# A tower of two mixture-of-experts layers on one core: side-by-side spreads and plain turns in the second experts, a few steps moved between engines

## What is computed

```python
h = tokens(x)        # interpolate by 4, windows of 64, |FFT| of a polynomial and a gaussian, soft minimum
h = h + attention0(layernorm(h))
h = h + experts0(layernorm(h))      # 16 experts, top 2
h = h + attention1(layernorm(h))    # 8 heads with a positional part
h = h + experts1(layernorm(h))      # 8 experts, top 2, gelu; its core:
logits = tokens @ router_w.T;  probs = softmax(logits);  rw, re = top_k(probs, 2);  rw = rw / rw.sum()
combine = zeros(N, 8).at[rows, re].set(rw)
for e in range(8):
    y = gelu(tokens @ w1[e] + b1[e]) @ w2[e] + b2[e]
    out = out + combine[:, e:e+1] * y      # out starts as tokens
```

## Time and profile before

| | |
|---|---|
| time, three runs | 739.51 us (738.17 to 740.50) |
| the profiled execution | 737.55 us, of which the span from first to last instruction is 735.8 us |
| mean granted PE clock | 0.983 |
| PE | 645.7 us busy (88%), 5070 matmuls |
| DVE | 570.9 us (78%) |
| ACT | 502.1 us (68%) |
| POOL | 334.1 us (45%) |
| L1861 and L1839 | 18.0 us each in the second experts |
| L1851 / L1874 | 9.6 us / 8.8 us |

### The profile page before, as it was taken

One profiled execution on the slowest core, in us unless ns is written; L12 is line 12 of the kernel. 1 busy time (PEld: TensorE's weight loads), 2 busy tenths in 40 slices (PEclk: granted clock), 3 DMA queues, 4 the chain that ended last, 5 costly groups with the idle time before them and its releaser, 6 DMA issues. The chain is left out here.

```text
span 735.8 us, 16590 instructions
## 1 busy us (share of the span) xinstructions
PE 645.7 (88%) x5070; PEld 353.0 (48%) x5070; DVE 570.9 (78%) x1647; ACT 502.1 (68%) x1264; POOL 334.1 (45%) x417
## 2 busy tenths in 40 slices
PE   4557998999999988899999988799888988888896
PEld 4524655666666653233332224455555655553332
DVE  6677787777777775899999989779988888867653
ACT  2747877888888872677777767658777777745542
POOL 1007678688787885223232334725445644320000
PEclk9869999999999999999999999999999999999998
DMA  4030000000000001633233330000000000000011
GB/s 111 1 114 1 2 2 0 0 0 0 0 0 0 1 1 47 204 100 108 96 116 115 110 109 16 2 2 1 1 0 0 0 0 0 2 1 2 15 22 22
DMA packets 22038, 24.37 MB, mean 33 GB/s; under 512 B 12390, under 2 KB 12902, under 8 KB 21734
## 3 DMA queue, kind: packets, MB, share of 16 engines
q1 hardware_dynamic: 19751, 23.31, 10.5%
q10 hardware_dynamic: 2239, 0.49, 0.3%
HBM read 22.48 MB, written 1.31 MB: 32 GB/s over the span
## 5 line engine op out<-in xcount | busy, mean ns | idle before, releaser
L1358 POOL TENSOR_TENSOR big<-big 128x1024 f32<-128x1024 f32 x64 | 119.8, 1893 | 44.2 <-DVE big L1172 44.2
L956 ACT ACTIVATE big<-ps,big 128x255 f32<-128x255 f32 x256 | 117.0, 483 | 10.0 <-DVE big L1166 7.5
L918 ACT ACTIVATE big<-ps,b1s 128x512 f32<-128x512 f32 x128 | 80.1, 678 | 31.1 <-PE ps L650 30.0
L1166 DVE TENSOR_REDUCE big<-ps 128x4 f32<-128x1020 f32 x64 | 75.1, 1212 | 25.0 <-PE ps L726 25.0
L1962 ACT ACTIVATE big<-ps 128x1024 f32<-128x1024 f32 x64 | 65.9, 1030 | 33.1 <-PE ps L1589 30.7
L2104 DVE TENSOR_REDUCE big<-ps 128x4 f32<-128x1020 f32 x64 | 78.0, 1219 | 6.9 <-DVE res L2161 2.5
L732 PE MATMUL ps<-cst,big 128*128 128x128 f32 x512 | 76.7, 283 | 6.3 <-POOL big L1358 2.4
L1178 DVE COPY mid<-ps 128x512 f32<-128x512 f32 x96 | 63.4, 685 | 18.3 <-PE ps L732 15.1
L732 PEld LDWEIGHTS ps<-cst,big 128*128 128x128 f32 x512 | 54.2, 140 | 40.8 <-issue 21.5
L650 PE MATMUL ps<-big,wall 64*128 64x512 f32 x256 | 72.1, 640 | 0.7 <-ACT big L889 0.7
L661 PE MATMUL ps<-big,w2s 128*64 128x512 f32 x256 | 69.0, 617 | 3.1 <-ACT big L918 1.8
(11 more groups left out here) (276 smaller groups left out, 1329.9 us busy)
## 6 DMA issues: line engine op xcount, KB each, us to landing
mid<-spread_w SPq DMA_DIRECT2D x128, 128.0 KB, 2.8
mid<-in_split_sel SPq DMA_DIRECT2D x1, 1536.0 KB, 7.0
wall<-in_w SPq DMA_DIRECT2D x1, 1280.0 KB, 6.1
out_tokens<-res SPq DMA_DIRECT2D x16, 56.0 KB, 1.6
cst<-in_consts SPq DMA_DIRECT2D x1, 520.5 KB, 4.9
pexp<-in_w_raw SPq DMA_DIRECT2D x1, 512.0 KB, 6.5
w2s<-in_w SPq DMA_DIRECT2D x1, 512.0 KB, 3.4
mid<-in_taps ACTq DMA_DIRECT2D x1, 320.0 KB, 3.9
```

Of the source, the lines that this page charges most:

```text
L918: last = nc.scalar.activation(hid[e % 2][j], H1(e, j), ACT.Relu, bias=b1s[0][:, 2 * e + j:2 * e + j + 1])
L956: last = nc.scalar.activation(e_sb[r % 4][:, jj, tq, 0:NW], S[:, 2 * (r % 2) + jj, tq, 0:NW], ACT.Exp, scale=-1.0, bias=minus[r % 4][:, jj ...
L1166: nc.vector.tensor_reduce(minus[r % 4], S[:, 2 * a:2 * a + 2, :, 0:NW], AX.X, ALU.min).then_inc(s_mx, 1)
L1358: nc.gpsimd.tensor_tensor(e_sb[r % 4], e_sb[r % 4], bc(inverse[r % 4].unsqueeze(3), [P, 2, 2, 256]), ALU.mult).then_inc(s_A, 1)
```

## The change

1. *Spreads.* `selb` holds its rows twice, at partitions 0 and 32, with 32 rows each (24 and 8 of zeros). The matmul of pair n takes partitions 32n to 32n+31 of `selb` and of `ct`.
2. *Sums.* `sum_turn` is four transposes of 128 x 128 in place of four matmuls with `fold`. PSUM then holds the two halves side by side, and `finish` adds them in one more DVE instruction.
3. *Tokens.* The absolute value moves to ACT (activation Abs), ahead of each exp. The mirrored columns are no longer a second subtraction on DVE but a copy on ACT of those in `res`, read backwards.
4. *Averages.* `averages(others)` over 24 tiles becomes one over 12 tiles (part 1) in the same place and one over the last 12 after `normed(1)`; `centre(1)` goes ahead of `inverse_roots(0)`.
5. *Stores.* SP's loop ends one chunk earlier; of the last chunk's four DMAs SP issues the two of tq = 0 and ACT the two of tq = 1.

```diff
-        selb = sb("selb", [3 * 8, 4, P], BF16)
+        selb = sb("selb", [2 * 32, 4, P], BF16)
...
                     for t in (0, 1):
+                        act.wait_ge(s_dist, t + 1)
+                        nc.scalar.activation(arg[:, t], mask[:, t], ACT.Abs).then_inc(s_abs, 1)
                         act.wait_ge(s_abs, t + 1)
                         nc.scalar.activation(arg[:, t], arg[:, t], ACT.Exp, scale=-1.0).then_inc(s_exp, 1)
...
                     nc.scalar.activation(lo[D:P], raw[D:P], ACT.Copy).then_inc(s_cast, 1)
+                    for t in (0, 1):
+                        act.wait_ge(s_half, t + 1)
+                        nc.scalar.activation(rows[:, t, :, NB:WIN], rows[:, t, :, NB - 2:0:-1], ACT.Copy).then_inc(s_mirror, 1)
                     act.wait_ge(s_cast, 1)
+                    act.wait_ge(s_mirror, 2)
...
-                        link(nc.vector.scalar_tensor_tensor(out=mask[:, t], in0=over(t), scalar=-BETA, in1=mt[:, t], op0=ALU.mult, op1=ALU.add))
-                        nc.vector.scalar_tensor_tensor(out=arg[:, t], in0=mask[:, t], scalar=-1.0, in1=mask[:, t], op0=ALU.mult, op1=ALU.max).then_inc(s_abs, 1)
+                        nc.vector.scalar_tensor_tensor(out=mask[:, t], in0=over(t), scalar=-BETA, in1=mt[:, t], op0=ALU.mult, op1=ALU.add).then_inc(s_dist, 1)
...
-                        link(nc.vector.tensor_tensor(rows[:, t, :, 0:NB], low[:, t], arg[:, t], ALU.subtract))
-
-                        link(nc.vector.tensor_tensor(rows[:, t, :, NB:WIN], low[:, t, :, NB - 2:0:-1], arg[:, t, :, NB - 2:0:-1], ALU.subtract))
+                        nc.vector.tensor_tensor(rows[:, t, :, 0:NB], low[:, t], arg[:, t], ALU.subtract).then_inc(s_half, 1)
+                    dve.wait_ge(s_half, 2)
...
                 averages(PREP[0])
                 centre(0)
-                averages(others)
+                averages(PREP[1])
                 variances(0, PREP[0])
+                centre(1)
                 inverse_roots(0, PREP[0])
                 dve.wait_ge(s_cen, 1)
                 normed(0)
                 normed(1)
-                centre(1)
+                averages(PREP[2])
                 centre(2)
...
+            def store(eng, c, tq):
+
+                eng.wait_ge(s_done, c + 1)
+                for first, n in ((0, 112), (112, 16 - tq)):
...
-                        last = nc.tensor.matmul(CB(n), selb[:, 2 * g + n], ct[0:PART, c], start=True, stop=True)
+                        copy = slice(32 * n, 32 * n + 32)
+                        last = nc.tensor.matmul(CB(n), selb[copy, 2 * g + n], ct[copy, c], start=True, stop=True)
...
-                        last = nc.tensor.matmul(YT[:, D * k:D * k + D], y_sb[:, P * k:P * k + P], fold[:], start=True, stop=True)
+                        last = nc.tensor.transpose(YT[:, P * k:P * k + P], y_sb[:, P * k:P * k + P], ident)
...
                 y_out(CH - 1)
+                store(act, CH - 1, 1)
...
-                    y = YT[:, 0:TC * D].rearrange("p (t d) -> p t d", t=TC)
+                    y = YT.rearrange("p (t j d) -> p t j d", t=TC, j=2)
...
-                    link(nc.vector.tensor_tensor(yy, y, x2[:, tl, 0], ALU.add))
+                    link(nc.vector.tensor_tensor(yy, y[:, :, 0], x2[:, tl, 0], ALU.add))
+                    link(nc.vector.tensor_tensor(yy, yy, y[:, :, 1], ALU.add))
...
-                with sp.Fori(0, CH) as c:
-                    store(c)
+                with sp.Fori(0, CH - 1) as c:
+                    for tq in range(2):
+                        store(sp, c, tq)
+                store(sp, CH - 1, 0)
```

More of the change, by code:

```diff
@@ L201, in tokens @@
             s_m2, s_mag, s_arg, s_mask = sem("tok_power_sum"), sem("tok_mag"), sem("tok_arg"), sem("tok_mask")
-            s_abs, s_exp, s_log = sem("tok_abs"), sem("tok_exp"), sem("tok_log")
+            s_dist, s_abs, s_exp, s_log = sem("tok_distance"), sem("tok_abs"), sem("tok_exp"), sem("tok_log")
+            s_half, s_mirror = sem("tok_first_columns"), sem("tok_mirrored_columns")
+            rows = res[:].rearrange("p (b t) d -> p t b d", t=2)
             s_w32 = sem("tok_fp32_weights_in")
@@ L336, in _ @@
                         link(nc.vector.tensor_tensor(mt[:, t], mag[:, t], mask[:, t], ALU.mult))
-                        link(nc.vector.scalar_tensor_tensor(out=mask[:, t], in0=over(t), scalar=-BETA, in1=mt[:, t], op0=ALU.mult, op1=ALU.add))
-                        nc.vector.scalar_tensor_tensor(out=arg[:, t], in0=mask[:, t], scalar=-1.0, in1=mask[:, t], op0=ALU.mult, op1=ALU.max).then_inc(s_abs, 1)
+                        nc.vector.scalar_tensor_tensor(out=mask[:, t], in0=over(t), scalar=-BETA, in1=mt[:, t], op0=ALU.mult, op1=ALU.add).then_inc(s_dist, 1)
                     for t in (0, 1):
                         link(nc.vector.scalar_tensor_tensor(out=low[:, t], in0=over(t), scalar=BETA, in1=mt[:, t], op0=ALU.mult, op1=ALU.min))
-                    rows = res[:].rearrange("p (b t) d -> p t b d", t=2)
                     for t in (0, 1):
                         dve.wait_ge(s_log, t + 1)
-                        link(nc.vector.tensor_tensor(rows[:, t, :, 0:NB], low[:, t], arg[:, t], ALU.subtract))
-                        link(nc.vector.tensor_tensor(rows[:, t, :, NB:WIN], low[:, t, :, NB - 2:0:-1], arg[:, t, :, NB - 2:0:-1], ALU.subtract))
+                        nc.vector.tensor_tensor(rows[:, t, :, 0:NB], low[:, t], arg[:, t], ALU.subtract).then_inc(s_half, 1)
+                    dve.wait_ge(s_half, 2)
                 @block.gpsimd
@@ L1353, in output_biases @@
                     link_p(nc.gpsimd.tensor_tensor(b2p[64:96], rest_b[64:96], md[64:96], ALU.subtract))
-                    link_p(nc.gpsimd.tensor_copy(selb[0:24].rearrange("p e f -> p (e f)"), cst[0:24, o_sel1:o_sel1 + 4 * P]))
+                    link_p(nc.gpsimd.tensor_copy(selb[:].rearrange("p e f -> p (e f)"), cst[0:64, o_sel1:o_sel1 + 4 * P]))
                 def weigh(r, R):
@@ L1526, in attention1_and_experts1 @@
             E = 8
-            PART = 3 * E
             half = NT // 2
@@ L1546, in logit_columns @@
                 return ps[:, LOGIT_BANKS[c][r], first:first + n * E].rearrange("p (t e) -> p t e", t=n)
+            def store(eng, c, tq):
+                eng.wait_ge(s_done, c + 1)
+                for first, n in ((0, 112), (112, 16 - tq)):
+                    src = res[first:first + n].rearrange("p (b t) d -> p b t d", t=2)
+                    eng.dma_start(out[bass.ds(2 * c, 2), P * tq + first:P * tq + first + n].rearrange("b w d -> w b d"),
+                                  src[:, bass.ds(2 * c, 2), tq]).then_inc(s_out, 16)
             turned_weights = lambda d: ps[0:96, WEIGHT_BANK[d // 2], 256 * (d % 2):256 * (d % 2) + 256].bitcast(BF16)
@@ L2429, in _ @@
             def _(sp):
-                def store(c):
-                    sp.wait_ge(s_done, c + 1)
+                with sp.Fori(0, CH - 1) as c:
                     for tq in range(2):
[L2433 to L2436, removed]
-                with sp.Fori(0, CH) as c:
-                    store(c)
+                        store(sp, c, tq)
+                store(sp, CH - 1, 0)
                 sp.wait_ge(s_out, 16 * 4 * CH)
@@ L2492, in constant_table @@
     sel1 = np.zeros((P, 4, 2, 64))
-    for part in range(3):
-        for e in range(8):
-            sel1[8 * part + e, e // 2, e % 2] = 1
+    for row in (0, 32):
+        for part in range(3):
+            for e in range(8):
+                sel1[row + 8 * part + e, e // 2, e % 2] = 1
     neg = np.zeros((P, 1))
```

## The result

The changed kernel takes 735.58 us (median of 8 runs, 732.39 to 737.01), the kernel before 740.00 beside it (8 runs, 736.42 to 745.06): a ratio of 0.993, 95% interval 0.990 to 0.996. Forecast were 733.6 and a range of 731.5 to 736.6. The profiled execution took 734.33 us, with a span of 732.5.

The account below looks back on a forecast made before the run. PE was taken to bound the second experts, its groups running without a gap. Gains of 4.2 (second experts), 1.05 (stores), 0.4 (tokens) and 0.2 (averages) sum to 5.9 us: 739.5 to 733.6, range 731.5 to 736.6.

Parts of the forecast that it names:

- Spreads: Paired 512-column matmuls in the second experts overlap on two 32-row groups: 0.53 to 0.32 us, a gain of 0.21 each.
- Sum turns and chunk: Steady chunks, second experts: sum turn 1.03 to 0.59 us, chunk 6.44 to 5.58, 0.3 of DVE's idle left.
- Rival 2: Second experts: DVE or the engines' loops bind, not PE; 1.5 us lost in all, 735.1 us; chance 0.1.
- The third add at 694: Before weigh(3, 0), where DVE has no idle, finish(1)'s extra add costs its 0.45 us on the path.
- the step by step sum: Second experts, running gain: 1.1 at table change, 0.8 after third add, 1.4, 4.0 after chunk 6, 4.2 us at end.
- "1.1" up to the table change: Second experts' start: three spreads and one sum turn, less 0.1 for routing waits, plus 0.1 from spread (0, 0).
- The tail: Second experts' end: spread (7, 1) and sum turn 6 give nothing; the last sum turn's 0.44 offsets the add's 0.45.
- Last stores: Kernel's end: the last chunk's four DMAs on two queues; 1.15 us less 0.1 for SP's queue, gain 1.05.
- Rival 3: Last stores and tokens' end: ACT issues slowly or reads backwards slowly; 1.0 to 1.9 us less, 735.1; chance 0.08.
- Tokens' end: Tokens' block: work moved to ACT; table change behind the first Abs costs 0.35 us, yet the end gains 0.4.
- rival 4: Steady chunks, second experts: PE, too idle, falls to its lower clock; slower, at about 745 us; chance 0.05.
- a change of another stage by more than 0.5 us: Sign that the prediction is wrong: a stage the change doesn't touch, attention 0 or 1, changes length by over 0.5 us.

Follow-up runs that it names:

- only_turns: The kernel before with only the plain sum turns and the third add: 740.91 us (one run).
- only_stores: The kernel before with only the last stores split over two queues: 740.13 us (one run).
- before_again: The kernel before, unedited, profiled and timed once more: 739.28 us (10 runs), ratio 0.997 to 19 runs of the same kernel beside it.
- after_third: The changed kernel, without further edit, a third time: 736.70 us (7 runs), ratio 0.992 to the kernel before.
- after: The changed kernel with all five parts, first measurement: 735.58 us (8 runs), ratio 0.993 to the kernel before.
- after_again: The changed kernel, without further edit, once more: 734.33 us (10 runs), ratio 0.992 to the kernel before.
- only_spreads: The kernel before with only the side-by-side spreads, first of two such runs: 744.6 us (one run).

## Why the prediction was right

**Spreads**: 0.53 to 0.32, as read off the paired matmuls of attention 1; 2.66 us on the path against 2.3 and the 0.1 of spread (0, 0).

**Sum turns and chunk**: 0.59, 5.57 and an idle of 0.30 on DVE, all three as worked out. Rival 2 fell.

**The third add at 694**: on the path, as told; 0.34 more from `finish(1)` to `weigh(3, 0)`, and from spread (3, 0) to spread (3, 1) 0.45 more than with the spreads alone (5.14 against 4.69), 0.33 more than in a kernel before without a fall (4.81), where 0.35 was worked out.

**The second experts in all**: the step by step sum (1.1, 0.8, 1.4, 4.0, 4.2) against spread (7, 0), 4.92 us earlier where 4.0 stood, and 5.1 at the last add where 4.2 stood. Of the 0.9 too much, 0.67 is the fall of the clock at 694, which the profiled execution of before happened to have and the changed one has not; the forecast took the stage of before as it stood, with its fall in it. The rest is a mis-sized term: "1.1" up to the table change measured 1.30 (spread (2, 1) comes 15.16 us behind the first one, 16.46 before). Of these, the spreads alone bring 0.85 and the turns alone 0.45, once the falls are taken out of their profiles, so the two savings simply add. Spread (0, 0) brought its whole 0.22 (2.97 us to the next spread before, 2.75 now) where 0.1 stood, and the 0.1 set aside for the waits for the routing was not lost.

**The tail**: forecast at nothing, and it is nothing: the last add ends 6.46 us behind spread (7, 1) in both kernels.

**Last stores**: 0.91 for 1.05, from the last add to the end. The 0.1 that the forecast took back for SP's queue of chunk 6 is there, 0.15 in only_turns and 0.09 between only_stores and the changed kernel. Rival 3's slow issue didn't come: 0.92 us for two, not 1.85 for one.

**Tokens' end**: 0.4 forecast. The second sigmoid, up to which nothing was changed, comes at 33.72 in the profile of before, the latest of all fourteen, and at 33.47 in the changed one's: 0.24 of the 1.13 us is chance. Measured against it, the block's end comes 0.5 earlier, and DVE starts 0.4 nearer to it. The first is the sum's step, with its table change behind the first Abs just where it was placed (0.3 against 0.35; the terms given there make 39.02 - 38.63 = 0.39). The Trainium skill ("ScalarE: Activation LUTs", Table sets) is borne out in that: the load at 35.54 belongs to exp, and the first Abs at 34.88 needed none. Its drain of 1.38 us beside each load is shown by no row here either: exp starts at the end of its 1.28 us load. The second, the barrier, wasn't in the forecast: that 0.4 is luck.

**Averages**: 0.15 for 0.2.

**The clock, rival 4**: its place was the steady chunks, and there it didn't come: in none of the fourteen profiles does a fall lie between spread (4, 0) and the last add. Ahead of it, where PE waits for the routing, falls come with and without the change (6.8 us at 695 in before_again and at 698 in after_third, none in after and after_again). What took most of the gain of the first pair (7.3 us locally, 3.25 in the span) is the clock in attention 0. The prediction named a change of another stage by more than 0.5 us as a sign that it is wrong. The sign came (3.13 in attention 0) and was badly chosen: a stage that the change doesn't touch moves by 3 us between two executions of one program. Over the three comparisons the medians lie 4.4, 7.1 and 5.2 us apart, where 5.9 was forecast.

**The predicted time**, 733.6, lies 2.0 under the median. The saving was sound; the base was the median of three runs, 739.51, and the medians of 8 to 19 runs of the same kernel are 739.3 to 741.9. That the span of after_again, 729.0, is so near to the 729.9 of the sum is in part luck: the base had 0.67 us of a fall and 0.24 of a late sigmoid in it, and the barrier gave 0.4 that wasn't counted; against these, attention 0 and the first experts took 0.3 us more each. What remains open is what makes the clock fall in one execution and not in the next.

## What to carry to other kernels

Where a stage is PE's row of groups without a gap, price an edit by the distance of group starts, and write beside it what idle time of the next engine it eats: here both came out within 0.02 us of a chunk. Before two profiles are compared, list the falls of the clock in both and take each out by the same distance in an execution without it; a stage's length with a fall in it, be it in its first half microsecond, is no base. When a step moves to ACT for room, ask what stands ahead of a table change: half of this step gained, the other half cost 0.3 us, and by one profile of each, moving only the copies would have been better.

## What the runs showed of the hardware

Behind the barrier the engines don't start together. Where DVE came last, its first instruction stands 0.45 us behind SP's; where ACT came last, DVE's stands 0.04 behind. That being last is the cause isn't shown: the six profiles of the second kind all have the edit at the tokens' end too. ACT pays nothing of the sort: its first step, a table change, starts 0.01 us behind SP's whether it came last (44.01 and 44.00) or not (44.73 and 44.72).

In only_spreads the clock stayed at 0.50, the lower level of 1.2 GHz, for 17.10 us, of which PE was busy 16.82. The falls have places (about 68, 115, 314, 436, 670 and 697 us; thirteen of the fourteen profiles have at least one), but which of them comes differs between executions. Falls at 313 to 316 go with first experts of 165.9 to 167.4 us, against at most 163.8 without. Without any fall this stage took 160.4 to 162.8, for which no cause was found.

Two bf16 matmuls of 512 columns on two groups of 32 rows take the time of one: 0.39 us from the first start to the last end, where a single matmul of that size has a mean of 378 ns in the kernel before.
